# A recurrent scan with a mixture of experts on one core: expert numbers put into PE's registers amid the preceding tile's products, and a new order of the front's steps, of the second scan pass and of the loads

## The chip, the cores and the metric

The kernel runs on one core of one Trainium2 chip. The metric is the device time in microseconds of one execution, as the median over several. The engines are PE (TensorE: matrix products and transposes), DVE (VectorE), ACT (ScalarE), POOL (GpSimd) and SP (which here only issues transfers). Each has its own instruction stream, which it works off in order, and they meet only over semaphores: an instruction waits until a counter has reached a value, and others raise it.

## The reference

The input is x of 2 sequences with 2048 positions of 256 values: 4096 rows, 32 tiles of 128. The first part is a recurrence over time with a layer norm behind it, the second a gated expert layer with a layer norm behind it.

```
# part 1
xB = einsum('bsd,nd->bsn', x, B)
state = tanh(state @ A.T + xb_t)                  # over all positions, states kept
out = einsum('bsn,dn->bsd', states, C) + D * x
attn = layernorm(out + x) * gamma + beta
x = layernorm(x + attn)
# part 2: 8 experts in 2 groups, one group chosen, of it the best 2 experts
scores = sigmoid(x @ router_weight.T);  choice = scores + correction_bias
group = argmax over groups of the sum of the two largest choices
topk = the two best experts of that group;  w = scores[topk] / sum
routed = sum over the two of w * ((silu(x @ w_gate[e]) * (x @ w_up[e])) @ w_down[e])
shared = (silu(x @ sw_gate) * (x @ sw_up)) @ sw_down
x = layernorm(x + routed + shared)
```

## The kernel before, in words

*Scan.* The 4096 positions are cut into 128 chunks of 32 positions that run side by side, so a step of the scan is one matrix product for all chunks (`scan_step`: `drive` puts the B product of the next step into a PSUM bank, the A product is added, ACT takes the tanh). A first pass over 32 steps gives each chunk's starting state, and a second pass of 32 steps, from those, gives the states. During the first pass PE also turns the tiles of x. At step `WMAX_AT` it turns the maxima of the weights that DVE has found, from which come the powers of two by which the weights are scaled before they are split into two f16 parts.

*Front.* The 32 tiles are 8 groups of 4. Every engine walks through one list of tokens, `PLAN`, made by `plan()`, and does those that are its own; so the list sets the order on each engine, and semaphores do the rest. For a group g (with halves n = 2g and 2g+1):

- `A` (PE, `project`): C and D products into PSUM. `M` (DVE, `first`): their statistics. `r` (POOL): root. `S` (DVE, `scaled`), `B` (DVE, `normed`): scale, add the residual, statistics. `R` (POOL): root.
- `X` (ACT, `second`, two halves): second norm and rounding to f16. `Y` (DVE, `low`): the low f16 part. `T` (PE, `turn_x2`): transposes. `K` (ACT, `keep_x2`): copy out of PSUM.
- `L` (PE, `logits`), `Q` (ACT, `squash`), `D` (DVE, `choose`: which two experts), `P` (PE, `ranks`), `E` (DVE, `slots` and `weigh`: the row's place in the sorted list, and its weights), `V` (POOL, four scatters of the rows to DRAM).
- the shared expert, for each half: `U` (PE, `up`), `s` (ACT, `silu`), `H` (DVE, `inner`), `W` (PE, `down`), `Z` (DVE, `add_shared`). All `W` write one bank, so `down(n)` waits for `Z` n-1.

Before, tokens of groups 0 and 1 were put between steps of the second scan pass by a table (`early`), and then period p took `A M r S B R X` of group p, `Y` to `Z` of group p-1, and `P E V` of group p-2.

*Expert tiles.* Rows are sorted by their pair of experts. `N` (DVE, `table`) makes a table that gives for each of up to 43 tiles its first row (`tabR`) and its two experts (`tabE`). SP loads the rows of each tile from DRAM. In iteration i of the list PE does `u` (`up_tile`) of tile i-1, `v` (`turn_h`) of i-2, `t` (`turn_tile`) of i, `d` (`down_tile`) of i-3; ACT does `us` (`silu_tile`) of i-1, `ve` (`keep_h`) of i-2, `te` (`keep_tile`) of i, and then the final scaling `o`. Buffers and banks are double. For a pair of tiles in `ENDS` the last norm is done together: `rr` is POOL's root chain and `os` its scatter of finished rows. The number of an expert is data, so the address of its weights comes from a register of PE that `value_load` fills from SBUF: for both ranks in `up_tile` and again in `down_tile`, each time before the first product:

```
def pair_of(j):
    return [pe.value_load(tabE[0:1, r, j:j + 1], min_val=0, max_val=E - 1) for r in range(2)]
```

Behind the tiles stand slow paths that run only if the chunks' states have not met, and are not run here.

## Time and profile before

| | us |
|---|---|
| median of 3 runs (461.68 to 467.6) | 463.37 |
| profiled execution, its own time | 460.74 |
| its span, first to last instruction | 459.0 |
| PE busy | 299.2 (65%) |
| DVE busy | 236.1 (51%) |
| ACT busy | 155.3 (34%) |
| POOL busy | 139.3 (30%) |
| mean granted TensorE clock | 0.904 of full speed |

The rows further down come from one profiled execution. A row of the timeline or of the chain names a start and a duration in us, the engine, the line of the kernel and what was written from what; in brackets stands the idle time of the engine before it, and what ended it. PEld is PE's loading of weights into the array, PEldq its sequencer's own instructions, which don't count as busy. "issue" is time in which nothing that the profile shows was waited for. The granted clock is 1.00 at 2.4 GHz and 0.50 at 1.2 GHz; a value between is a mean over both.

### The profile page before, as it was taken

To read this page: it belongs to the slowest core of one execution; us is meant where nothing else is said; L and a number is where in the kernel's file an instruction comes from. 1 tells how busy PE (TensorE), PEld (TensorE's weight loads), DVE (VectorE), ACT (ScalarE), POOL (GpSimd) and SP (SyncE) were. 2 spreads that over 40 slices of the span, in tenths; PEclk is the share of its full clock that TensorE was granted. 3 is DMA by queue.
4 is the path that set the end of the run, shared out by engine and by line. 5 is a ranking of instruction groups with operands and counts; after the bars stand their busy time and mean duration, and the time that the engine had idled before them with its cause. 6 is when DMAs were issued, how large, how long until landed. Compare 5 with 4: busy or idle time off the path is not lost.

```text
span 459.0 us, 7930 instructions
## 1 busy us (share of the span) xinstructions
PE 299.2 (65%) x2237; PEld 238.5 (52%) x2237; DVE 236.1 (51%) x928; ACT 155.3 (34%) x354; POOL 139.3 (30%) x241
## 2 busy tenths in 40 slices
PE   6889988737466667665603766667666666766640
PEld 5789977635354546454502645455554545555430
DVE  3259944384948676686491244444344444434440
ACT  2444246123232423324101243443534344353420
POOL 2200111051615152342330024333342333334353
PEclk9999999997887978888755799999999999999995
DMA  6994000010202020211227413223222323300000
GB/s 210 311 361 164 1 0 1 0 66 29 95 0 96 0 95 1 94 43 52 94 94 212 118 33 108 72 81 98 82 76 85 101 71 88 87 22 33 28 5 1
DMA packets 21002, 36.82 MB, mean 80 GB/s; under 512 B 3028, under 2 KB 9693, under 8 KB 20960
## 3 DMA queue, kind: packets, MB, share of 16 engines
q1 hardware_dynamic: 16336, 23.50, 17.6%
q0 software_dynamic: 4624, 12.79, 7.4%
q8 instruction: 23, 0.38, 0.3%
q14 instruction: 19, 0.16, 0.1%
HBM read 20.00 MB, written 17.71 MB: 82 GB/s over the span
## 4 chain that ended last, share of the span: by engine, by line
PE 58%; issue 19%; DVE 7%; ACT 5%; SPq 4%; DMA 3%; POOL 2%; POOLq 0%; DVEq 0%; ACTq 0%
PE bank L657 15%; PE bank L678 10%; PE bank L610 7%; PE bank L622 5%; PE bank L516 4%; PE bank L521 3%; PE bank L557 3%; PE bank L554 3%; PE bank L569 2%; PE bank L633 2%; PE bank L669 2%; ACT xT L797 2%; DMA rows<-in_L_attn_x_dram 2%; SPq L420 1%; DVE rows L1169 1%
## 5 line engine op out<-in xcount | busy, mean ns | idle before, releaser
L657 PE MATMUL bank<-w,xTt 128*128 x516 | 66.8, 281 | 29.3 <-issue 29.3
L657 PEld LDWEIGHTS bank<-w,xTt 128*128 128x128 f16 x516 | 47.2, 100 | 53.2 <-issue 46.5
L678 PE MATMUL bank<-wd,thT 128*128 x172 | 49.3, 410 | 34.6 <-issue 34.6
L1362 POOL TENSOR_TENSOR rstd<-mv,eps 128x2 f32<-128x2 f32 (+2 forms) x39 | 10.0, 258 | 203.3 <-DVE mv L1202 95.4
L821 ACT ACTIVATE tsg<-bank,g_un 128x256 f32<-128x256 f32 x43 | 20.4, 474 | 117.7 <-PE bank L657 117.7
L1395 POOL DMA_INDIRECT out_dram<-xT,where x43 | 44.1, 1025 | 44.4 <-ACT xT L833 36.2
L1188 DVE SCALAR_TENSOR_TENSOR th_<-bank,tw,tsg 128x128 f32<-128x128 f32 x86 | 26.2, 346 | 59.1 <-ACT tsg L821 45.4
L678 PEld LDWEIGHTS bank<-wd,thT 128*128 128x128 f32 x172 | 29.6, 192 | 44.4 <-issue 42.0
L622 PE MATMUL bank<-wd,h 128*128 128x256 f32 x64 | 23.2, 496 | 35.3 <-issue 15.2
L1381 POOL DMA_INDIRECT xs_dram<-rows,slot_i x32 | 33.8, 1056 | 40.8 <-DVE rows L1094 27.9
L1196 DVE TENSOR_TENSOR xT<-bank,xT 128x256 f32<-128x256 f32 x43 | 18.3, 424 | 53.9 <-PE bank L678 53.9
L516 PE MATMUL bank<-xT,BT 128*128 128x128 f32 x256 | 40.3, 281 | 0.0
L610 PE MATMUL bank<-xT,w 128*128 128x256 f16 x192 | 36.3, 364 | 0.0
L1366 POOL TENSOR_TENSOR rstd<-rstd,neghalf 128x2 f32<-128x2 f32 (+2 forms) x39 | 34.9, 894 | 0.6
L516 PEld LDWEIGHTS bank<-xT,BT 128*128 128x128 f32 x256 | 34.5, 196 | 0.1
L622 PEld LDWEIGHTS bank<-wd,h 128*128 128x128 f32 x64 | 13.3, 230 | 40.4 <-DVE h L1163 23.3
L815 ACT ACTIVATE xTt<-bank 128x512 f16<-128x512 f16 x43 | 25.7, 598 | 21.1 <-PE bank L633 20.2
L797 ACT ACTIVATE xT<-bank 128x1024 f16<-128x1024 f16 x16 | 16.4, 1024 | 41.8 <-PE bank L569 41.8
L610 PEld LDWEIGHTS bank<-xT,w 128*128 128x128 f16 x192 | 25.2, 133 | 9.5 <-issue 1.6
L633 PE MATMUL bank<-ident,xT 128*128 128x128 f16 x172 | 17.4, 226 | 14.4 <-DMA xT<-xs_dram 14.4
L833 ACT ACTIVATE xT<-xT,rstd 128x256 f32<-128x256 f32 x43 | 23.7, 604 | 7.9 <-POOL rstd L1372 7.9
L809 ACT ACTIVATE sg<-bank,g_un 128x256 f32<-128x256 f32 x16 | 7.6, 474 | 49.3 <-PE bank L610 49.3
(180 smaller groups left out, 531.5 us busy)
## 6 DMA issues: line engine op xcount, KB each, us to landing
xT<-xs_dram SPq DMA_DIRECT2D x43, 262.0 KB, 3.0
rows<-in_L_attn_x_dram SPq DMA_DIRECT2D x7, 512.0 KB, 7.2
xs_dram<-cmp SPq DMA_DIRECT2D x1, 3144.0 KB, 12.9
...
out_dram<-xT,where POOLq DMA_INDIRECT x43, 2.4
...
xs_dram<-rows,slot_i POOLq DMA_INDIRECT x32, 2.8
...
```

What stands on the lines that cost most here:

```text
L516: pe.matmul(ps_scan[s % 2][:, 0:P], BT[:, k, :], xT[:, k, tile, :], start=(k == 0), stop=False)
L610: last = pe.matmul(ps_gu(n)[:, i * 2 * P:(i + 1) * 2 * P], w16[:, pw, E, k, i, :], cols[:, px, k, :], start=(m == 0), stop=(m == 3 * KT - 1))
L622: last = pe.matmul(ps_y[:, t * DM:(t + 1) * DM], h[:, n % 3, t * P:(t + 1) * P], wd[:, E, :], start=True, stop=True)
L633: last = pe.transpose(ps_tx(j)[:, a, k, :], row[:, a, k * P:(k + 1) * P], ident16[:, :])
L657: last = pe.matmul(ps_tu(j)[:, r, :, :].rearrange("p w i -> p (w i)"), xTt[:, j % 2, 2 * px + k, :], w16[:, pw, bass.ds(e, 1), k, :, :].re ...
L678: last = pe.matmul(ps_ty(j), thT[:, j % 2, r, :], wd[:, bass.ds(e, 1), :].rearrange("p o d -> p (o d)"), start=(r == 0), stop=(r == 1))
L797: nc.scalar.activation(x2cols(g)[:, :, :, half * 2 * P:(half + 1) * 2 * P], x2_turn[:, :, :, :], ACT.Copy).then_inc(x2_kept, 1)
L815: nc.scalar.activation(xTt[:, j % 2, :, :], ps_tx(j).rearrange("p a k t -> p (a k) t"), ACT.Copy).then_inc(tx_kept, 1)
L1188: stt(th_[:, j % 2, r, :], ps_tu(j)[:, r, 1, :], tw[:, j % 4, r:r + 1], tsg[:, j % 2, r, :], ALU.mult, ALU.mult).then_inc(th_ready, 1)
L1366: ins = nc.gpsimd.tensor_tensor(scale[:, 1, :], scale[:, 0, :], neghalf[:, 0:n], ALU.pow)
L1381: nc.gpsimd.indirect_dma_start(out=xs_dram, out_offset=bass.IndirectOffsetOnAxis(ap=slot_i[:, l:l + 1], axis=0), in_=rows[:, l, :], in_off ...
L1395: nc.gpsimd.indirect_dma_start(out=out_rows, out_offset=bass.IndirectOffsetOnAxis(ap=where[:, j:j + 1], axis=0), in_=trow(j)[:, DM:2 * DM] ...
```

## The change

1. *Registers.* `pair_of` is gone. `know(j)` loads one of the two expert numbers of tile j. Only for the first tile both are loaded at the start of `up_tile`; every other tile's numbers are loaded in `up_tile` of the tile before, one ahead of the fourth of six products of either rank. `down_tile` uses the same registers.
2. *Plan.* The second scan pass is interleaved with the steps of groups 0 and 1 and nearly the whole of period 2, one short piece of the list ("atom") after each scan step. The order within a period is new. `weigh` has a token of its own, `w`, directly behind `D`. `A` of the next group stands at the end of a period. The check that the chunks have met is moved out of the scan to the end of period 4.
3. *Banks.* All shared ups use bank 6 and wait for the inner product of the half before; before, they took banks 0 and 1 in turn.
4. *Ends.* Tiles are paired until at most one is left, so the last three tiles end as a pair and one, and not as three.
5. *Loads and preparation.* New order of SP's transfers (vectors, C and router weights before the third group of x; x groups ahead of the weights; D late), of DVE's weight preparation and residual sums, of the D work on POOL, and the two steps at which PE turns the weights' maxima (19 and 21 instead of 15 and 19).

```diff
-        while len(js) > 3:
+        while len(js) > 1:
...
-        early = {4: [("A", 0), ("M", 0), ("r", 0)], 5: [("S", 0), ("B", 0), ("R", 0)], 12: [("A", 1), ("M", 1), ("r", 1)],
-                 15: [("X", 0, 0)], 17: [("X", 0, 1)], 19: [("Y", 0, 0), ("Y", 0, 1), ("S", 1)],
-                 20: [("T", 0, 0), ("K", 0, 0), ("B", 1), ("R", 1)], 22: [("T", 0, 1), ("K", 0, 1)], 24: [("L", 0), ("Q", 0)],
-                 25: [("D", 0)], 27: [("X", 1, 0)], 29: [("X", 1, 1)]}
-        for i in range(L):
-            put(("scan", i), *early.get(i, []))
...
+        steps = [("scan", i) for i in range(L)]
+
+        def scan(n=1):
+            put(*steps[:n])
+            del steps[:n]
+
+
+        scan(4)
+        put(("A", 0), ("M", 0), ("r", 0), ("S", 0), ("B", 0), ("R", 0))
+        scan(4)
+        put(("A", 1), ("M", 1), ("r", 1), ("S", 1))
+        scan(3)
+        put(("X", 0, 0))
+        scan(2)
+        put(("X", 0, 1), ("Y", 0, 0), ("T", 0, 0), ("K", 0, 0), ("Y", 0, 1))
+        scan(1)
+        put(("T", 0, 1), ("K", 0, 1), ("B", 1), ("R", 1))
+        for atom in ([("U", 0), ("s", 0)], [("L", 0), ("Q", 0), ("H", 0)], [("U", 1), ("s", 1), ("D", 0), ("w", 0), ("H", 1)],
+                     [("W", 0), ("Z", 0)], [("X", 1, 0)], [("A", 2)], [("X", 1, 1)], [("W", 1), ("Z", 1)]):
+            scan()
+            put(*atom)
+
+        def period(p):
 
             g, o = p - 1, p - 2
-            tiles = list(tiles)
-
-            def some(k, of):
-                for it in tiles[len(tiles) * k // of:len(tiles) * (k + 1) // of]:
-                    put(*it)
-            if p < G:
-                put(("A", p), ("M", p), ("r", p))
-            if g < G:
-                put(("Y", g, 0), ("T", g, 0), ("K", g, 0), ("Y", g, 1))
-            if 0 <= o < G:
-                put(("P", o), ("E", o))
-                put(*[("V", o, t) for t in range(T4)])
-            some(0, 4)
-            if p < G:
-                put(("S", p))
-            if g < G:
-                put(("T", g, 1), ("K", g, 1))
-                shared(2 * g)
-            if p < G:
-                put(("B", p), ("R", p))
-            some(1, 4)
-            if g < G:
-                put(("H", 2 * g), ("L", g), ("Q", g))
-                put(("W", 2 * g))
-                shared(2 * g + 1)
-                put(("D", g), ("H", 2 * g + 1), ("W", 2 * g + 1), ("Z", 2 * g))
-            some(2, 4)
-            if p < G:
-                put(("X", p, 0), ("X", p, 1))
-            if g < G:
-                put(("Z", 2 * g + 1))
-            some(3, 4)
-
-        queue = []
-        for n in range(2):
-            shared(n)
-            put(("H", n), ("W", n), ("Z", n))
-        for p in range(2, G + 2):
-            take = queue[:len(queue) // (G + 2 - p)] if p < G + 1 else queue
-            queue = queue[len(take):]
-            period(p, take)
-            for c, (g, _) in enumerate(CHECKS):
-                if g == p - 2:
-                    loads(c)
-                    queue += list(iterations(c))
-        for it in queue:
-            put(*it)
+            n = 2 * g
+            on, end = p < G, p >= G
+            atoms = []
+            if on:
+                atoms.append([("M", p), ("r", p)])
+            atoms += [[("P", o)], [("Y", g, 0), ("T", g, 0), ("K", g, 0)], [("Y", g, 1), ("T", g, 1), ("K", g, 1)]]
+            atoms.append([("E", o)] + [("V", o, t) for t in range(T4)])
+            if on:
+                atoms.append([("S", p)])
+            atoms += [[("U", n), ("s", n)], [("L", g), ("H", n), ("Q", g)], [("U", n + 1), ("s", n + 1)]]
+            if on:
+                atoms.append([("B", p), ("R", p)])
+            if end:
+                atoms += [[("W", n), ("D", g)], [("H", n + 1)], [("w", g), ("Z", n)], [("P", g), ("W", n + 1)],
+                          [("E", g), ("Z", n + 1)] + [("V", g, t) for t in range(T4)]]
+            else:
+                atoms += [[("W", n), ("H", n + 1)], [("D", g), ("w", g)], [("W", n + 1)]]
+                if p + 1 < G:
+                    atoms.append([("A", p + 1)])
+                atoms += [[("X", p, 0), ("X", p, 1)], [("Z", n)], [("Z", n + 1)]]
+            return atoms
+
+        for p in range(2, G + 1):
+            for atom in period(p):
+                if steps:
+                    scan()
+                put(*atom)
+            if p == 4:
+                put(("meet", 0))
...
-            return bank[n % 2 if n < two_banks else 0]
+        ps_gu = bank[6]
...
-        TURN_C_AT, WMAX_AT = 5, 15
+        TURN_C_AT, WMAX_AT = 5, 19
...
-            sp.dma_start(D_bc[:, :], D.partition_broadcast(P)).then_inc(D_in, 16)
-            sp.dma_start(D_col[:, :], D.rearrange("(k p) -> p k", p=P), allow_slow_non_contiguous=True).then_inc(D_in, 16)
-            load_x(2)
-            sp.dma_start(C_sb[:, :, :], C.rearrange("(k p) n -> p k n", p=P)).then_inc(Cr_in, 16)
-            sp.dma_start(rw_sb[:, :], router_weight).then_inc(Cr_in, 16)
-            load_weights(0)
-            load_x(3)
-            load_weights(1)
-            load_x(4)
-            load_x(5)
             sp.dma_start(gamma_bc[:, :], gamma.partition_broadcast(P)).then_inc(vecs_in, 16)
             sp.dma_start(beta_bc[:, :], beta.partition_broadcast(P)).then_inc(vecs_in, 16)
             sp.dma_start(cbias_bc[:, :], correction_bias.partition_broadcast(P)).then_inc(vecs_in, 16)
+            sp.dma_start(C_sb[:, :, :], C.rearrange("(k p) n -> p k n", p=P)).then_inc(Cr_in, 16)
+            sp.dma_start(rw_sb[:, :], router_weight).then_inc(Cr_in, 16)
+            load_x(2)
+            load_x(3)
+            load_weights(0)
+            load_x(4)
+            load_weights(1)
+            load_x(5)
+            sp.dma_start(D_bc[:, :], D.partition_broadcast(P)).then_inc(D_in, 16)
+            sp.dma_start(D_col[:, :], D.rearrange("(k p) -> p k", p=P), allow_slow_non_contiguous=True).then_inc(D_in, 16)
...
-                if n >= 1 and (n >= two_banks or n >= 2):
-                    pe.wait_ge(h_done, n if n >= two_banks else n - 1)
+                if n:
+                    pe.wait_ge(h_done, n)
...
-            def pair_of(j):
-                return [pe.value_load(tabE[0:1, r, j:j + 1], min_val=0, max_val=E - 1) for r in range(2)]
+            pair = {j: [] for j in range(NT)}
+
+            def know(j):
+
+                pair[j].append(pe.value_load(tabE[0:1, len(pair[j]), j:j + 1], min_val=0, max_val=E - 1))
 
             def up_tile(j):
 
                 if j == starts[check_of[j]]:
                     pe.wait_ge(table_ready, check_of[j] + 1)
+                    know(j)
+                    know(j)
...
-                for r, e in enumerate(pair_of(j)):
+                for r, e in enumerate(pair[j]):
                     m = 0
                     for k in range(KT):
                         for pw, px in ((0, 0), (0, 1), (1, 0)):
+                            if m == 3 and j + 1 < starts[check_of[j] + 1]:
+                                know(j + 1)
...
+            dve.wait_ge(vecs_in, 16 * NVEC)
+            residual(0)
+            residual(1)
             dve.wait_ge(Cr_turned, 1)
             nc.vector.tensor_copy(rwT[:, :, :].rearrange("p k n -> p (k n)"),
                                   ps_mats[1][:, KT * P:KT * P + KT * E]).then_inc(Cr_done, 1)
             nc.vector.tensor_copy(CT[:, :, :].rearrange("p k n -> p (k n)"),
                                   ps_mats[1][:, 0:KT * P]).then_inc(Cr_done, 1)
-            def residual(n):
-
-                dve.wait_ge(xT_turned, T4 * (n + 1))
-                tt(xres[:, n * T4:(n + 1) * T4, :], xres[:, n * T4:(n + 1) * T4, :],
-                   beta_bc[:, :].unsqueeze(1).to_broadcast([P, T4, DM]), ALU.add).then_inc(res_done, 1)
-
+            residual(2)
             dve.wait_ge(Cr_done, 2)
             greatest(2)
-            for i in (0, 1):
-                dve.wait_ge(w_in[i], 16 * 2)
-                greatest(i)
+            dve.wait_ge(w_in[0], 16 * 2)
+            greatest(0)
+            residual(3)
+            dve.wait_ge(w_in[1], 16 * 2)
+            greatest(1)
+            residual(4)
             scales()
-            dve.wait_ge(vecs_in, 16 * NVEC)
-            for done, i in enumerate((2, 0, 1)):
-                split(i, done + 1)
-                residual(2 * done)
-                residual(2 * done + 1)
+            split(2, 1)
+            split(0, 2)
+            residual(5)
+            split(1, 3)
...
+                elif kind == "w":
+                    weigh(n)
                 elif kind == "E":
                     slots(n)
-                    weigh(n)
```

In PE's instruction stream, at a tile of the middle. L633 (L628 after) are the transposes of `t`, L637 (L635) the register loads, L678 `d`, L657 `u`; ISA rows are register instructions. Before:

```order
L633 MATMUL bank<-ident,xT 128x128 x3
L637 TENSOR_LOAD tabE [waits z2_done,th_kept]
L637 ISA x2
L637 TENSOR_LOAD tabE
L637 ISA x2
L678 ISA
L678 MATMUL bank<-wd,thT 128x256
L678 ISA
L678 MATMUL bank<-wd,thT 128x256
L637 TENSOR_LOAD tabE [waits th_ready,tx_kept]
L637 ISA x2
L637 TENSOR_LOAD tabE
```

The same place in the change:

```order
L628 MATMUL bank<-ident,xT 128x128 x3
L678 ISA [waits z2_done,th_kept]
L678 MATMUL bank<-wd,thT 128x256
L678 ISA
L678 MATMUL bank<-wd,thT 128x256
L657 ISA [waits th_ready,tx_kept]
L657 MATMUL bank<-w,xTt 128x256 x2
L657 ISA
L657 MATMUL bank<-w,xTt 128x256
L635 TENSOR_LOAD tabE
L635 ISA x2
L657 ISA
```

The four loads of a tile that stood before `d` and `u` have become two, each behind three products of `u`; the waits are now on the register instructions of `d` and `u` themselves.

In DVE's stream, in a period of the front: L1060 ends `choose`, L1163 is `inner`, L1169 `add_shared`, L978 the statistics of `first`. Before:

```order
L1059 TENSOR_REDUCE code<-coded 128x4 [waits choice_step]
L1060 TENSOR_TENSOR pick<-code,codes 128x48 [waits choice_step]
L1163 SCALAR_TENSOR_TENSOR h<-bank,u_un,sg 128x256 [waits down_done,silu_done]
L1169 TENSOR_TENSOR rows<-bank,rows 128x2x256 [waits down_done] x2
L978 BN_STATS st<-bank 128x6 [waits c_done]
```

In the change (all lines are 7 further down; L1096 to L1101 are `weigh`; the `inner` of the same half stands 16 rows further up, before `choose`):

```order
L1067 TENSOR_TENSOR pick<-code,codes 128x48 [waits choice_step]
L1096 TENSOR_SCALAR score<-th 128x32
L1097 TENSOR_TENSOR score<-score,kept 128x32 [waits weigh_step]
L1098 TENSOR_REDUCE total<-score 128x4 [waits weigh_step]
L1099 TENSOR_SCALAR total<-total,u_inv 128x4 [waits weigh_step]
L1100 RECIPROCAL total<-total 128x4 [waits weigh_step]
L1101 TENSOR_TENSOR rows<-score,total 128x4x8 [waits weigh_step]
L1176 TENSOR_TENSOR rows<-bank,rows 128x2x256 [waits down_done] x2
L985 BN_STATS st<-bank 128x6 [waits c_done]
```

`choose` and `weigh` have come between the second `inner` and the first `add_shared` of a group.

In PE's stream, at the end of a period: L610 (L605 after) is `up`, L581 `logits`, L622 (L617) `down`, L554 (L549) the start of `project`. Before:

```order
L581 MATMUL bank<-rw,xT 128x8 x23
L622 MATMUL bank<-wd,h 128x256 [waits zbase_done,h_done]
L622 MATMUL bank<-wd,h 128x256
L610 MATMUL bank<-xT,w 128x256 [waits x2_kept,h_done]
L610 MATMUL bank<-xT,w 128x256 x11
L622 MATMUL bank<-wd,h 128x256 [waits zbase_done,h_done]
L622 MATMUL bank<-wd,h 128x256
L554 MATMUL bank<-CT,states 128x256 [waits scan_tanh,scaled1]
```

In the change:

```order
L605 MATMUL bank<-xT,w 128x256 [waits x2_kept,h_done]
L605 MATMUL bank<-xT,w 128x256 x11
L617 MATMUL bank<-wd,h 128x256 [waits zbase_done,h_done]
L617 MATMUL bank<-wd,h 128x256
L617 MATMUL bank<-wd,h 128x256 [waits zbase_done,h_done]
L617 MATMUL bank<-wd,h 128x256
L549 MATMUL bank<-CT,states 128x256 [waits scan_tanh,scaled1]
```

Both downs of a group now stand behind its second up, and `project` directly behind them.

## Rows read from the trace of the kernel before

**Rows 1.** Busy time by stretch: from:to, length, each engine (instructions), clock, DMA share, GB/s

```profile
0.00:42.46 42.46, 35.03 (x274) 32.97 (x275) 20.94 (x80) 18.05 (x62) 5.43 (x26) 1.00 0.90 283
42.46:82.11 39.65, 35.06 (x279) 31.20 (x278) 24.48 (x75) 16.97 (x47) 5.65 (x12) 1.00 0.00 1
82.11:114.90 32.79, 20.62 (x158) 16.73 (x155) 19.02 (x73) 7.45 (x13) 7.97 (x10) 0.90 0.09 33
114.90:198.20 83.30, 53.16 (x416) 42.37 (x416) 57.21 (x233) 26.02 (x44) 31.21 (x40) 0.84 0.14 53
198.20:243.53 45.33, 19.12 (x168) 14.64 (x168) 31.81 (x124) 9.79 (x16) 16.07 (x18) 0.71 0.21 79
243.53:262.25 18.72, 11.71 (x60) 8.29 (x61) 2.98 (x16) 4.33 (x9) 0.00 (x0) 0.60 0.62 185
262.25:436.13 173.88, 119.08 (x859) 88.61 (x859) 74.59 (x314) 68.76 (x155) 63.10 (x114) 1.00 0.25 70
436.13:459.00 22.87, 5.40 (x29) 3.72 (x29) 5.03 (x20) 3.90 (x8) 9.85 (x21) 0.72 0.02 3
```

**Rows 2.** Line 637: durations in ns (least, median, most), first and last start

```profile
L637 PEldq TENSOR_LOAD <-tabE x172: 293/301/491, 245.0 to 441.6; - x172
L637 PEldq FUSED_REGOPS  x172: 151/151/165, 245.6 to 442.0; - x172
```

**Rows 3.** Timeline of two expert tiles, ACT and PE

```profile
312.72 0.47 ACT L821 ACTIVATE tsg<-bank,g_un 128x256 f32<-128x256 f32 x1 [3.03 <-PE bank L657]
...
313.36 0.60 ACT L815 ACTIVATE xTt<-bank 128x512 f16<-128x512 f16 x1
...
315.56 1.48 PE L657 MATMUL bank<-w,xTt 128*128 x12 [0.54 <-issue]
...
318.05 0.60 ACT L815 ACTIVATE xTt<-bank 128x512 f16<-128x512 f16 x1 [0.23 <-PE bank L633]
```

**Rows 4.** Timeline of the second scan pass, ACT

```profile
50.06 0.28 ACT L769 ACTIVATE states<-bank 128x128 f32<-128x128 f32 x1 [3.90 <-PE bank L521]
50.92 0.28 ACT L769 ACTIVATE states<-bank 128x128 f32<-128x128 f32 x1 [0.58 <-PE bank L521]
...
62.12 1.08 ACT L789 ACTIVATE rows<-w,rstd 128x256 f32<-128x256 f32 x2
```

**Rows 5.** Chain that ended last, a stretch of one period

```profile
135.08 0.76 DVE st L978 x2
...
136.12 0.59 DVE rows L1007
...
137.41 1.03 ACT xT L797
...
138.58 0.71 PE bank L569 x8
```

**Rows 6.** The chain in the last tiles, on POOL

```profile
445.43 0.21 POOL rstd L1362
...
447.27 1.08 POOL out_dram L1395
...
448.38 0.20 POOL rstd L1362
```

**Rows 7.** Timeline of the first scan pass, PE

```profile
24.27 0.44 PE L506 MATMUL bank<-ident,rows 128*128 128x128 f32 x2 [3.25 <-DMA rows<-in_L_attn_x_dram]
```

**Rows 8.** The chain in the period before, DVE

```profile
117.39 0.09 DVE score L1089
...
118.63 1.58 DVE w L986 x4
...
120.33 1.67 DVE w L995 x4
...
123.60 0.38 DVE h L1163
```

**Rows 9.** Timeline of a period, DVE's choose and PE's second down

```profile
145.05 0.18 DVE L1013 SCALAR_TENSOR_TENSOR choice<-th,chbias_bc 128x32 f32<-128x32 f32 x1
...
147.62 0.21 DVE L1060 TENSOR_TENSOR pick<-code,codes 128x48 f16<-128x48 f32 x1
...
151.06 1.10 PE L622 MATMUL bank<-wd,h 128*128 128x256 f32 x4 [1.77 <-DVE rows L1169]
```

46 lines of the change are left out of this document (25 added, 21 removed).

## Prediction

> **What bounds the kernel now.** I read the busy time by stage first [rows 1]. There is a front (two passes of a scan, then groups of four tiles, then a table) up to 243.53 us, and then 43 expert tiles. From 262.25 to 436.13 us 39 tiles pass in 173.88 us, 4.46 us each, at the full granted clock (2.4 GHz); PE is busy for 119.1 of it, DVE for 74.6, ACT for 68.8, POOL for 63.1, the DMA engines at 0.25. No engine is full, so I look for a chain. The register loads of `pair_of` are 172 TENSOR_LOADs of 301 ns, each followed by register arithmetic of 151 ns [rows 2]: four a tile, all in PE's sequencer, which works in order. In the timeline [rows 3] ACT ends the copy of the next tile's rows (L815) at 313.96, and the products L657 that read it start at 315.56: 1.60 us, filled by the two loads of `up_tile`. The products take 1.48 (to 317.04), and the next L815 ends at 318.65. So there is a ring: copy ended, two loads, 12 products, three activations on ACT, copy ended. `down_tile` has two more loads, between the transposes and L678.
>
> In the front the clock is 1.00 through the scans, and 0.84 as a mean of 1.2 and 2.4 GHz in the four periods from 114.90 to 198.20 [rows 1]; these take 20.83 us each, with PE busy 13.3 and DVE 14.3. They too are a chain over engines. The second scan pass takes 39.65 us for 32 steps. A step costs 0.86 (ACT's 0.28 and 0.58 idle), and what stands between two steps is added: `project` 3.3 (an idle of 3.90 instead of 0.58), an `X` half about 1.0 (two L789 are 1.08), a T/K half about as much (K is 1.03, mostly ahead of the next step) [rows 4, 5].
>
> **The tile stage.** *Loads.* One load is at least 0.30 + 0.15 = 0.45 us and at most 0.80, half of the 1.60 [rows 2, 3]. I take 0.64, since what is left of the 1.60 must also hold two hand-overs. The change removes two of four loads and puts the other two behind product 3 of each rank. There they are no longer ahead of the products; but PE has only three of them in hand when a load begins (0.33 us, 12 taking 1.3 and a tail), so it runs dry. The hole is at most the whole load, 0.64, and at least 0.64 - 0.33 = 0.31. Handing three over takes nearly as long as working them, so I take 0.48. The 12 products then take 1.48 + 2 x 0.48 = 2.44.
>
> *The ring after.* Copy ended to first product without a load: 0.14, as from L797's end, 138.44, to the transposes at 138.58 [rows 5]. Products 2.44. Then ACT: 1.24 from its first activation in one tile (312.72 to 313.96), 1.61 from the products' end in the next (317.04 to 318.65) [rows 3]; mean 1.42. Sum 4.0. The sequencer alone would need 4.46 - 2 x 0.64 = 3.2, PE's own work 119.1 / 39 = 3.05: the ring still sets the time, through ACT. Saved 0.46 a tile, 39 x 0.46 = 17.9 us. Holes of 0.31 and 0.64 make the ring 3.7 and 4.3, savings of 30 and 6.
>
> *The first tiles*, 243.53 to 262.25, have the clock at 0.60 [rows 1]. At 1.2 GHz three products take 0.65, as long as a load, so the holes nearly close and most of the 1.3 of two loads is saved, two to three times: 2.8, between 1.5 and 4.
>
> *The end.* The last three tiles are single ends; from the root chain of one (445.43) to that of the next (448.38) are 2.95 us, the send's 1.08 among them [rows 6]. With tiles 40 and 41 as a pair one root chain (1.9) goes, and the sends of 38 and 39 no longer stand behind it. PE's last tiles lose three pairs of loads, in part under the same chain. Of 22.9 us I take 4.3; 2 to 5.
>
> **The front.** *Loads.* PE waits 3.25 us for x rows in the first pass [rows 7]: the fifth group, which stood behind both gate and up weights. It now stands ahead of the 1.15 MB of up weights, which at 0.283 MB/us [rows 1] are 4 us: this wait goes. The sixth group stays behind as many bytes as before, and PE comes to it 3.2 sooner, with part of four steps as slack: some 1.5 of wait returns. Net 1.8, between 0 and 3. The scale products move from step 15 to 19, and wait for the up weights' maximum; the sixth group of x, for which step 16 waits, is issued behind those weights, so I count them as there; if not, PE and the scan stop. D lands later, but D_diag is needed only by project 0, in the second pass, and costs nothing. `residual` moves forward into DVE's waits for weights; that is the cover for project 0 a step earlier, and without it Y 0 and with it the scan come late by up to a project, 3.3. On POOL only the D work moves behind the iotas, which nothing waits for here.
>
> *The second pass* now also holds project 2 (3.3), two T/K halves (2.0), four shared-expert ups (12 products each, 1.3 less the step's slack of 0.2: 4.4), two downs (1.8), logits and ranks (0.7): 12.2 more, 51.9 if nothing overlaps. Project 2 on PE lies beside X 1.0 on ACT, and others likewise; I take 50. In exchange the stretch from the pass's end to the end of `first(3)`'s statistics, 82.11 to 114.90, shrinks to the rest of one period: B 3.27, H 0.5, D 2.8, w 1.24, Z 0.6, down 1.1, project 3.3, the last statistics 1.04 [rows 5, 8, 9], together 13.9, of which 2 lie in the pass. So 72.4 us become 62: 10.4 saved, 6 to 14.
>
> *The periods.* In the new order DVE does H 2g+1, D, w and only then Z 2g. `down` 2g+1 waits for that Z; project p+1 is queued behind this down on PE, and `first(p+1)` on DVE waits for project. The chain at full clock: statistics 1.04 (135.08 to 136.12), Y 0.6, T 0.7, K 1.03, T 0.7, up 1.3, silu 0.5, H 0.5, B 3.27, H 0.5, D 2.8 (145.05 to 147.83), w 1.24, Z 0.6, down 0.15 + 1.10, project 3.3. Sum 19.3. Before, D lay under the second up, and w under no wait of PE's. PE idles from the end of down 2g to Z 2g, about 5 us, where the same down now waits 1.77 [rows 9]. What follows at 1.2 GHz is down and part of project: 1.5 to 2.5. So 21.4 against 20.83: four periods cost 2.3 more; 19.5 to 23 gives -5 to +9.
>
> *The last group and the table*, 198.20 to 243.53, 45.3 us: w is done ahead of ranks, and slots ahead of the last Z, so the last scatter need not wait for w and slots (1.24 and about 1.0). I take 1.9 saved; -1 to 5.
>
> Sum: 1.8 + 10.4 - 2.3 + 1.9 + 2.8 + 17.9 + 4.3 = 36.8 us, from the profiled execution's span of 459.0 to 422.2. That execution took 460.74, 1.7 more than its span, and is 2.6 below the median of 463.37, whose three runs spread over 6; with 1.7 and half of 2.6 this gives **425 us**. Of the gain the sequencer and its ring are 21, the front 12, the end 4.
>
> **Rivals.**
> 1. *The front gives back what it gains.* The wait of some 5 us before down 2g+1 is followed by all of down and project at 1.2 GHz, and T and up after the wait for the statistics too: 19.3 + 2.5 + 1.7 = 23.5 a period, and the last group as much later. For it: clock 0.84 in the periods against 1.00 in the scans [rows 1]. Against: PE is dense from down through project. The four periods cost 10.7 instead of 2.3, the last group 3 more: 436. The Trainium skill (TensorE: Matmul & The Clock Gate, Loop structure matters more than you think) says that a long wait inside the loop lets PE go cold, which speaks against this order; by it the time would be this rival's 436.
> 2. *The loads are free amid the products*: PE works on while the sequencer loads. Products 1.48, ring 0.14 + 1.48 + 1.42 = 3.05, so the sequencer's 3.2 sets it: 39 x 1.26 = 49 saved instead of 18, 394. Against: the sequencer stops at `up_tile`'s start until the copy has ended, so nothing is queued ahead, and each product's weights are addressed from registers computed behind the load. The Trainium skill (Advanced Engine Details and Errata, Sequencer Loop) has it that other engine instructions can be read and queued while a control instruction executes; by that it would be 394. No row here has products behind a load that could show it.
> 3. *The loads only change place*: holes of 0.64 and slower handing over, the ring stays near 4.46 and the tile stage gives nothing: 443. For it: ACT's part of the ring is untouched, and both loads are still in it.
> 4. *The other side*: a load amid an accumulation waits until the products under way have drained. Each then costs 0.64, a product's 0.28 and a hand-over of 0.14 with no lead, 1.06: products 3.6, ring 5.2, 0.7 a tile or 28 us lost, against 19 gained elsewhere: 472. It decides against the kernel from a ring of 4.95 on (19 / 39 = 0.49 above 4.46). Against: in [rows 2] the loads' median is 301 and the least 293 ns, and the loads of `up_tile` stand directly behind L678's products; a drain would spread them.
>
> **How the numbers follow.** The forecast 0.62; rival 1 0.18; rival 2 0.05; rival 3 0.08; 1 and 3 together (454) 0.03; rival 4 0.04. Inside the forecast the unknown costs reach from holes of 0.31 (-12) to holes of 0.64 (+12) and periods of 23 (+7), not all at one end. To leave out no more than 2 in 10 I take in rival 1 and stop short of rival 3: 409 to 441. Faster by over 2% (about what a measurement of this kernel can tell from no change) 0.92, within 2% 0.04, slower 0.04.
>
> **What would show it.** 86 TENSOR_LOADs instead of 172; L657's 12 products in 2.2 to 2.8 us instead of 1.48, in three bursts; a tile in 4.0 us; no idle time before L678 that is put down to issue. In the front: no 3 us wait for x; the second pass's end near 91 us; a DVE sequence h, choose, weigh, Z with PE's down waiting 5 us for it in each period of 21.4. The forecast is wrong if the ring is under 3.5 (rival 2) or over 4.3 (rival 3), or if the first expert tile's transposes come after 240 (rival 1) or before 224.

## The result and the profile after

The changed kernel takes 435.54 us (median of 4 runs, 434.05 to 436.16) against 462.52 for the kernel before, run on the same chip: a ratio of 0.943, 95% interval 0.938 to 0.948. The forecast was 425 with a range of 409 to 441. So the sign and the range were right, and the middle was 10.5 us too low. The profiled execution has a span of 434.1 us and a mean granted clock of 0.885 of full speed, against 459.0 and 0.904.

The stages of the changed kernel, busy time by stretch with the columns of [rows 1]:

```profile
0.00:41.69 41.69, 35.39 (x274) 33.55 (x275) 24.95 (x83) 18.05 (x62) 6.84 (x26) 1.00 0.86 275
41.69:91.75 50.06, 46.51 (x405) 42.04 (x405) 32.53 (x111) 20.39 (x54) 11.71 (x18) 1.00 0.09 34
91.75:105.20 13.45, 7.64 (x39) 6.34 (x37) 7.18 (x40) 3.36 (x7) 1.70 (x4) 0.75 0.00 0
105.20:196.80 91.60, 52.29 (x416) 43.99 (x416) 57.09 (x235) 26.12 (x44) 30.72 (x40) 0.80 0.13 48
196.80:242.88 46.08, 19.22 (x160) 14.28 (x161) 30.49 (x116) 9.89 (x16) 15.81 (x18) 0.66 0.22 77
242.88:258.88 16.00, 12.11 (x61) 7.77 (x62) 2.78 (x15) 4.31 (x9) 0.00 (x0) 0.61 0.76 218
258.88:414.40 155.52, 124.39 (x860) 80.36 (x858) 74.38 (x312) 66.58 (x155) 63.09 (x114) 1.00 0.27 78
414.40:434.10 19.70, 5.13 (x29) 3.62 (x29) 5.50 (x21) 3.80 (x8) 8.68 (x17) 0.72 0.04 9
```

They stand against [rows 1] line by line: first pass, second pass, what lies from there to the end of `first(3)`, four periods, last group and table, first tiles, 39 tiles, end. The sum of the forecast, beside the measured stretches (us saved):

| term | forecast | measured |
|---|---|---|
| first scan pass | 1.8 | 0.8 (42.46 to 41.69) |
| second pass and the stretch behind it | 10.4 | 8.9 (72.4 to 63.5) |
| four periods | -2.3 | -8.3 (83.3 to 91.6) |
| last group and table | 1.9 | -0.8 (45.3 to 46.1) |
| first expert tiles | 2.8 | 2.7 (18.7 to 16.0) |
| 39 tiles | 17.9 | 18.4 (173.9 to 155.5) |
| end | 4.3 | 3.2 (22.9 to 19.7) |
| sum | 36.8 | 24.9 |

The ring of the tiles in the timeline of the changed kernel, PE and ACT; this answers to [rows 3]:

```profile
302.24 0.50 PE L657 MATMUL bank<-w,xTt 128*128 x3
...
303.13 0.83 PE L657 MATMUL bank<-w,xTt 128*128 x6 [0.39 <-issue]
...
304.34 0.50 PE L657 MATMUL bank<-w,xTt 128*128 x3 [0.38 <-issue]
...
304.88 0.47 ACT L822 ACTIVATE tsg<-bank,g_un 128x256 f32<-128x256 f32 x1 [2.78 <-PE bank L657]
...
305.51 0.60 ACT L816 ACTIVATE xTt<-bank 128x512 f16<-128x512 f16 x1
...
306.25 0.50 PE L657 MATMUL bank<-w,xTt 128*128 x3
```

The 12 products come in bursts of three, six and three, with a hole in front of the second and the third. They run from 302.24 to 304.84, 2.60 us instead of 1.48. ACT's three activations end at 306.11, and the next products start 0.14 later. A tile takes 4.01 here, 3.99 as a mean. Line 635, which is 637 of [rows 2], has half the loads, at the same duration:

```profile
L635 PEldq TENSOR_LOAD <-tabE x86: 295/302/488, 242.9 to 411.7; - x86
```

What PE and ACT waited for in the changed kernel (us in total, times, longest):

```profile
PE bank L617 <- DVE rows L1176: 39.9, 7, 7.0
PE bank L657 <- issue: 30.2, 78, 0.6
...
ACT th L803 <- remote: 17.6, 6, 3.8
```

L617 is `down`, L1176 is Z. The first line is the wait that the forecast foresaw at 5 us a period, behind choose and weigh. The third is one that it did not have: in six groups ACT stood waiting for the logits although PE's last product of them had ended. This wait for a semaphore that comes late is called the lag below. The kernel before has it too (L802 is the same tanh), 8.1 us in four groups:

```profile
ACT th L802 <- remote: 8.1, 4, 2.4
```

Three of these groups lie in its four periods, and the periods with the lag (20.6 to 20.9 us) are no longer than the one without it (21.2). In the changed kernel both waits are in the chain that ended last, here one period of it (start, us, what):

```profile
109.61 0.47 ACT sg L810
110.08 2.69 another core or an unknown queue
...
112.81 1.52 another core or an unknown queue
...
114.87 0.48 DVE h L1170
115.35 0.11 DVE choice L1020
...
119.29 0.61 DVE rows L1176
...
120.04 2.05 PE bank L617 x4
122.09 0.85 PE bank L549 x2
...
127.56 0.76 DVE st L985 x2
```

From h at 114.87 over choose and weigh (to 119.29), Z, and `down` at 120.04 to `project` from 122.09 to 127.54: that is the sequence of the forecast. `down` takes 2.05 instead of 1.10 [rows 9], `project` 5.45 where the forecast had 3.3 at full clock, and h comes about 1 us late (DVE was free from 113.8), because the logits' semaphore and that of the second up came late. "remote" in the list of waits and "another core or an unknown queue" in the chain name the same thing, a releaser that the profile doesn't find; the kernel has one core.

### The profile page after: what moved, and what is told of

Its sections match the earlier page's. It is cut to its first block, busy times and chain, and to the rows that moved or that the text cites. A ratio compares the mean times of both kernels' runs of the same rounds, so it can differ in the third digit from the quotient of the medians.

```text
span 434.1 us, 7668 instructions
## 1 busy us (share of the span) xinstructions
PE 302.7 (70%) x2237; PEld 231.9 (53%) x2237; DVE 234.9 (54%) x928; ACT 152.5 (35%) x354; POOL 138.6 (32%) x237
## 4 chain that ended last, share of the span: by engine, by line
PE 55%; DVE 14%; issue 12%; SPq 5%; ACT 4%; another core or an unknown queue 4%; DMA 3%; POOL 1%; POOLq 1%; DVEq 0%; ACTq 0%
PE bank L657 19%; PE bank L678 9%; PE bank L549 4%; PE bank L552 4%; PE bank L617 4%; PE bank L511 3%; SPq L415 3%; PE bank L516 3%; PE bank L605 2%; PE bank L628 2%; PE bank L669 2%; PE bank L564 2%; DVE rows L1176 1%; ACT xT L798 1%
## 5 line engine op out<-in xcount | busy, mean ns | idle before, releaser
L657 PE MATMUL bank<-w,xTt 128*128 x516 | 80.5, 282 | 35.0 <-issue 30.2
L657 PEld LDWEIGHTS bank<-w,xTt 128*128 128x128 f16 x516 | 39.7, 99 | 80.1 <-issue 74.5
L617 PE MATMUL bank<-wd,h 128*128 128x256 f32 x64 | 23.9, 510 | 39.9 <-DVE rows L1176 39.9
L678 PE MATMUL bank<-wd,thT 128*128 x172 | 47.7, 401 | 0.2 <-ACT thT L828 0.2
L617 PEld LDWEIGHTS bank<-wd,h 128*128 128x128 f32 x64 | 14.6, 253 | 44.2 <-issue 42.2
L798 ACT ACTIVATE xT<-bank 128x1024 f16<-128x1024 f16 x16 | 16.4, 1022 | 62.0 <-PE bank L564 62.0
L1375 POOL TENSOR_TENSOR rstd<-rstd,neghalf 128x2 f32<-128x2 f32 (+2 forms) x38 | 34.0, 896 | 0.6
L816 ACT ACTIVATE xTt<-bank 128x512 f16<-128x512 f16 x43 | 25.7, 598 | 18.7 <-PE bank L628 18.7
L678 PEld LDWEIGHTS bank<-wd,thT 128*128 128x128 f32 x172 | 29.8, 193 | 2.9 <-issue 0.6
L605 PE MATMUL bank<-xT,w 128*128 128x256 f16 x192 | 27.5, 300 | 2.9 <-DVE h L1170 2.5
L628 PE MATMUL bank<-ident,xT 128*128 128x128 f16 x172 | 17.4, 226 | 12.7 <-DMA xT<-xs_dram 12.7
L552 PEld LDWEIGHTS bank<-D_diag,xT 128*128 128x128 f32 x128 | 23.7, 230 | 3.0
L549 PE MATMUL bank<-CT,states 128*128 128x256 f32 x64 | 24.2, 467 | 0.0
```

The costliest lines, as they stand in the source:

```text
L549: pe.matmul(dst, states[:, g * T4 + t, :], CT[:, :, :].rearrange("p k d -> p (k d)"), start=True, stop=False, skip_group_check=True)
L552: last = pe.matmul(dst[:, k * P:(k + 1) * P], xT[:, k, g * T4 + t, :], D_diag[:, k, :], start=False, stop=(k == KT - 1), skip_group_check= ...
L605: last = pe.matmul(ps_gu[:, i * 2 * P:(i + 1) * 2 * P], w16[:, pw, E, k, i, :], cols[:, px, k, :], start=(m == 0), stop=(m == 3 * KT - 1))
L617: last = pe.matmul(ps_y[:, t * DM:(t + 1) * DM], h[:, n % 3, t * P:(t + 1) * P], wd[:, E, :], start=True, stop=True)
L628: last = pe.transpose(ps_tx(j)[:, a, k, :], row[:, a, k * P:(k + 1) * P], ident16[:, :])
L657: last = pe.matmul(ps_tu(j)[:, r, :, :].rearrange("p w i -> p (w i)"), xTt[:, j % 2, 2 * px + k, :], w16[:, pw, bass.ds(e, 1), k, :, :].re ...
```

## The experiments

Kernels of one call shared a chip and the runs of the kernel before: the first four (before 458.55 us), the next four (462.80), the next three (464.41), the last (460.48). Times are medians of 4 or 5 runs, or single runs where said. The parts of a profile (ring, periods, waits) are those of one execution of each kernel. A ratio to the kernel before carries from one call to another, where a difference of times does not.

**Run 1: the loads back at the heads.** Before each group of products two loads again, and none amid them:

```diff
-                for r, e in enumerate(pair[j]):
+                for r, e in enumerate(pair_of(j)):
...
-                            if m == 3 and j + 1 < starts[check_of[j] + 1]:
-                                know(j + 1)
...
-                for r, e in enumerate(pair[j]):
+                for r, e in enumerate(pair_of(j)):
```

> The changed kernel with one part undone: all four register loads of a tile stand again at the heads of its two groups of products, as in the kernel before; the front's new order, the loads of the inputs and the ends in pairs stay. Ring theory (two of four loads gone, the other two in holes of 0.55 us): the 39 tiles take 4.46 us each again instead of 3.99, so 18 us, the first tiles 2 to 3 more and the end about 1.5 more; the stage before the first expert tile is unchanged (first tile's transposes at 243 +- 1.5). Time 435.5 + 22 = 457, between 454 and 460. Rival (the tile stage got faster through something else of the change, above all the ends in pairs, which halve the root chains on POOL): the ring stays near 4.0 with four loads, the time under 445.

Measured: 451.69 us, ratio 0.986 (0.981 to 0.991), under the 454 to 460 expected. The ring is 4.45, from 253.6 (fourth tile) to 427.0 (last), the products take 1.48 again, and the end takes 20.6 instead of 19.7. PE's waits are back as they were (34.6 and 29.3 us before):

```profile
PE bank L678 <- issue: 34.6, 42, 1.1
PE bank L657 <- issue: 29.1, 43, 2.4
```

So the tile stage's gain is the registers': the ratio goes from 0.938 (the changed kernel in the next call) to 0.986, 22 us of 460. Run 4, in the same call and with the tiles of the changed kernel, is 22.1 under this run. At the end of the kernel the loads are 0.9 of the 3.2 us; the other 2.3 are left for the ends in pairs, which were not undone alone. One thing was not expected, and made the time miss its range: the stage before the first tile, whose code is unaltered, was 7 us shorter than in the changed kernel's own profile (236.0 instead of 242.9), and the lag was not in it.

Without the lag the four periods show what else is in them: they take 23.1, 21.0, 23.1 and 21.2 us. `down` takes 2.05 in each and `project` 4.5 to 5.3. The long ones have besides the first shared up at 1.2 GHz, here the first and the second period's in the chain:

```profile
106.68 2.57 PE bank L605 x12
...
129.47 1.32 PE bank L605 x12
```

**Run 2: the loads behind the down products.**

```diff
-                    know(j)
-                    know(j)
+                    for i in range(j, j + 3):
+                        know(i)
+                        know(i)
...
-                            if m == 3 and j + 1 < starts[check_of[j] + 1]:
-                                know(j + 1)
...
                 last.then_inc(ty_done, 1)
+                if j + 3 < NT:
+                    know(j + 3)
+                    know(j + 3)
```

Since a tile's numbers are now loaded three tiles ahead, those of the first three tiles are loaded together, six loads at the start of the first `up_tile`.

> The changed kernel with the two loads of a tile moved out of the up products to behind L678's products of an earlier tile, the down products, which take about 1.1 us of PE's time and for which nothing waits long. The 12 products L657 then have no load amid them. Theory A (the sequencer loads while PE still works on products it has in hand): products 1.48 us instead of 2.6; the loads begin when the last down product is handed over, about 0.3 to 0.5 us before it ends, and the next products start 0.8 to 1.0 later than the copy would let them; ring 3.5 to 3.85 us instead of 3.99, 6 to 19 us gained over 39 tiles, time 417 to 430. Theory B (a load waits until the products under way have drained): the loads begin when the down products have ended and take 1.3, ring 4.1 to 4.3, time 439 to 447. Theory C (the loads are not what makes the holes in the products, e.g. the change of expert costs it): products stay at 2.6.

Measured: 395.59 us, ratio 0.865 (0.859 to 0.871), some 35 us under the changed kernel (whose ratio is 0.938 to 0.943), better than any theory had it. In its own call it is 34 under run 4. The ring is 3.13 us. The timeline of one tile (lines are shifted: L656 is the up product, L677 the down product, L818 the copy), and under it the line of the loads in the window 303 to 305.4, times in ns, first and last start:

```profile
302.13 1.48 PE L656 MATMUL bank<-w,xTt 128*128 x12 [0.29 <-issue]
303.45 0.38 PE L668 MATMUL bank<-ident,th_ 128*128 128x128 f32 x2
303.67 0.39 PE L628 MATMUL bank<-ident,xT 128*128 128x128 f16 x4
303.89 1.08 PE L677 MATMUL bank<-wd,thT 128*128 x4
...
305.28 1.48 PE L656 MATMUL bank<-w,xTt 128*128 x12 [0.31 <-issue]
```

```profile
L635 PEldq TENSOR_LOAD <-tabE x2: 301/304/308, 303.7 to 304.4; - x2
```

The down products have register addresses as well, two pieces of arithmetic on them, done before the loads start:

```profile
L677 PEldq FUSED_REGOPS  x2: 46/46/46, 303.5 to 303.6; - x2
```

The first load starts at 303.7, when PE has four transposes and all four down products still to work, until 304.97. The second starts 0.65 later. Both are over just behind 305.0, when PE's work in hand ends too, and 0.1 to 0.2 behind the copy that ends at 304.88. So the sequencer was some 1.25 us ahead of PE, not 0.3 to 0.5 as theory A had it, and 1.3 us of loads cost 0.25: the products start 0.38 after the copy on the mean instead of 0.14. Theory B (a load drains the array) and theory C are out. PE's own stream is now the bound: its array is busy for 110.87 of the 122.1 us of the 39 tiles, and the other 11.2 are these holes of 0.29 behind the loads, for which it waits on no other engine.

**Run 3: Z first.** One step of DVE moved, in four periods:

```diff
-                atoms += [[("W", n), ("H", n + 1)], [("D", g), ("w", g)], [("W", n + 1)]]
+                atoms += [[("W", n), ("H", n + 1)], [("Z", n)], [("D", g), ("w", g)], [("W", n + 1)]]
...
-                atoms += [[("X", p, 0), ("X", p, 1)], [("Z", n)], [("Z", n + 1)]]
+                atoms += [[("X", p, 0), ("X", p, 1)], [("Z", n + 1)]]
```

> The changed kernel with one step moved in each of the four periods: on DVE the shared experts' sum Z 2g stands straight behind H 2g+1, ahead of choose and weigh, as it does nowhere in the two kernels. Theory of rival 1 (the loss in the periods comes from PE waiting 5 to 7 us before down 2g+1 for Z 2g behind choose and weigh, and from down, project and what follows at 1.2 GHz): the wait shrinks to under 2 us, down and project 3.3 to 3.6 us instead of 5.5, a period 17.5 to 19 us instead of 22.9, granted clock of the periods from 0.80 to 0.88 or more; time 416 to 420, 15 to 20 us less. Rival (the periods are bound by DVE's own work, or by the late logits and POOL's scatters, and the wait only moves): periods stay over 21.5 us and the time over 430.

Measured: 404.15 us, ratio 0.880 (0.874 to 0.885), 25.5 under run 4 where 15 to 20 were expected. First tile's transposes at 211.8. The four periods of run 1 (which has the changed kernel's front) and of this run, and this run's wait of PE:

```profile
103.30:191.70 88.40, 52.17 (x416) 43.66 (x416) 56.79 (x236) 26.45 (x44) 30.68 (x40) 0.81 0.13 50
```

```profile
98.90:169.40 70.50, 51.37 (x416) 41.52 (x416) 56.23 (x236) 26.47 (x44) 30.15 (x40) 0.81 0.16 62
```

```profile
PE bank L617 <- DVE rows L1176: 8.9, 7, 1.9
```

A period takes 17.6 instead of 22.1 us. The wait went from 34.7 us in seven (run 1) to 8.9. One `down` of a period, in run 1 and in this run:

```profile
118.49 2.04 PE L617 MATMUL bank<-wd,h 128*128 128x256 f32 x4 [5.82 <-DVE rows L1176]
```

```profile
145.97 1.10 PE L617 MATMUL bank<-wd,h 128*128 128x256 f32 x4 [0.87 <-DVE rows L1176]
```

In the four periods the wait is 5.8 each in run 1 and 1.1 on the mean here: 4.7 less, beside the 4.5 by which a period fell. `down` and `project` behind it are at full clock again (1.10 and 3.7). One part of the expectation was wrong: the mean clock did not rise (0.81 in both). Six of the eight shared ups of the periods now run at 1.2 GHz (2.6 to 2.8 us instead of 1.47), where in run 1 it was two of eight. So it is the wait that costs, and the slow clock has moved to other products.

**Run 4: the scatters behind the roots.**

```diff
-            atoms.append([("E", o)] + [("V", o, t) for t in range(T4)])
+            atoms.append([("E", o)] + ([] if on else [("V", o, t) for t in range(T4)]))
...
-                atoms.append([("B", p), ("R", p)])
+                atoms.append([("B", p), ("R", p)] + [("V", o, t) for t in range(T4)])
```

> The changed kernel with POOL's four scatters of a period moved behind its reciprocal roots R p, so that they no longer run while PE makes the logits and the second shared up. In the changed kernel the logits' semaphore comes 2.3 to 3.8 us later than the last recorded product of L in six groups, and ACT waits for it. Theory D (products of so few columns, or their hand-over, are slow while POOL's indirect DMAs run): the lag falls to about 0.3 us in the groups of the periods, silu 2g+1 and h 2g+1 come 0.9 to 1 earlier, the X halves that wait for R p up to 1 earlier; a period 21.5 to 22.3 instead of 22.9, time 431 to 434. Rival (the lag has another cause, and the scatters have none in it): lag stays over 2 us, time 435 +- 1.5.

Measured: 429.64 us, ratio 0.938 (0.933 to 0.943). Nothing can be read from it. None of the four kernels of this call has the lag, whether its scatters are moved or not, and the period of 22.1 is that of run 1 (22.25 in run 2).

**Run 5: the changed kernel again.**

> The changed kernel itself, beside the others of this call on the same chip, to be the base for them. In the four kernels run so far beyond it the logits' semaphore never came late, though two of them (loads at heads, loads behind down) have its front unaltered; in the changed kernel's own profile it came 2.3 to 3.8 us late in six groups, and so it did in the kernel before. If the lag belongs to the chip or the execution, this run has none, its four periods take 22.0 to 22.3 us instead of 22.9 and the first tile's transposes come at 236 to 238 instead of 242.9; time 428 to 432. If it belongs to the program, the lag and 22.9 are back, time 435 +- 1.5.

Measured: 433.78 us, ratio 0.938 (0.931 to 0.944), within 1% of the first call's 0.943. The lag is there (14.6 us in six groups), and the periods take 22.8. So it is no accident of one execution, and yet the same front ran without it in runs 1 and 2.

**Run 6: both edits.** Runs 2 and 3 together.

> The changed kernel with both edits that gained alone: the two register loads behind the down products (ring 3.13 instead of 3.99) and Z 2g ahead of choose and weigh (period 17.6 instead of 22.2). The two lie in different stages, one before 243 us and one behind. If they add: against the changed kernel on the same chip 34 us from the ring and the tail and 25 from the front, time 366 to 373. If the clock couples them (a denser front leaves a lower or higher clock to the tiles) they do not add, and the time is over 378.

Measured: 372.18 us, ratio 0.805 (0.800 to 0.810), 61.6 under run 5. They add: ring 3.13, period 17.7. The lag is there in five groups (11.3 us).

**Run 7: the loads behind the fifth product.** `m == 3` becomes `m == 5`.

> The changed kernel with its two loads amid the up products one place size further: behind the fifth of six products of each rank instead of the third. Theory H (handing a product to PE takes nearly as long as PE takes to work it, so the lead does not grow): the idle of PE behind the load stays at 0.5 to 0.6 us, the 12 products take 2.5 to 2.7 us, ring 3.9 to 4.05, time within 3 us of the changed kernel. Theory G (PE's sequencer gets ahead with each product, so five in hand cover more of the load than three): holes 0.1 to 0.4, products 1.7 to 2.3, ring 3.1 to 3.7, time 12 to 35 us less.

Measured, one run: 431.43 us, ring 3.96. The products in the timeline:

```profile
302.82 0.73 PE L657 MATMUL bank<-w,xTt 128*128 x5
303.94 0.84 PE L657 MATMUL bank<-w,xTt 128*128 x6 [0.39 <-issue]
305.12 0.28 PE L657 MATMUL bank<-w,xTt 128*128 x1 [0.34 <-issue]
```

Five, six and one, with holes of about the same size: the sixth product comes some 0.57 us later than it would without the load. So theory H holds: more products of this kind give almost no lead. The load starts at 303.2, when PE begins the fifth of the five products; in the changed kernel it starts as late, at 302.4, when PE begins the third of three. The line of the up products of the changed kernel has the sequencer's address arithmetic beside them:

```profile
L657 PE MATMUL bank<-w,xTt x516: 272/273/421, 244.7 to 415.6; 128*128 x172
L657 PEldq FUSED_REGOPS  x344: 46/46/51, 244.6 to 415.2; - x172
```

Each tile's 12 products carry 8 pieces of it. Run 2, where no load stands amid them, shows how fast the sequencer gets through them (one tile; first and last start):

```profile
L656 PE MATMUL bank<-w,xTt x12: 272/273/280, 305.3 to 306.5; 128*128 x12
L656 PEldq FUSED_REGOPS  x8: 46/46/51, 305.2 to 306.1; - x8
```

It gains about 0.3 us on PE over all twelve, so some 0.1 over three or five (an estimate from these two lines). Together with run 2 this settles what a load costs. Of its 0.65 to 0.77 us (0.65 from load to load in run 2; 1.55 for two at the heads of run 1, from 1.69 less 0.14), a hole of 0.56 is left amid the up products. Behind the down products two loads leave 0.24. The addresses of these come from registers as well, but they are done by 303.6 (run 2), and give PE 1.08 us of work.

**Run 8: both edits and Y first.** The steps Y g stand ahead of `first(p)` in each period.

> As the kernel with both edits, with one more step moved in the periods: Y g (both halves, the low parts of the second input) ahead of first p on DVE. In the kernel with Z first, PE stood from the end of project (97.6) to the transposes of g (99.6) and its first shared up came at 102.2 and at 1.2 GHz, since Y stood behind first's statistics, though the X that it reads had ended at 97.0. If that idle is what bounds the period now: transposes and up 1.5 to 3 us earlier and at full clock, a period 15.5 to 16.8 us instead of 17.6, time 4 to 9 us under the kernel with both edits. If first p with the root, the scaling and the normalisation behind it bound the period (they start 1.3 later here): no gain, or up to 1.3 us a period, 5 in all, lost.

Measured: 364.09 us, ratio 0.788 (0.782 to 0.794), 8.1 under run 6. The period is 15.4, though the lag is there in four groups (8.7 us).

**Run 9: with the scatters moved as well.** And the first tiles' loads are spread:

```diff
             def turn_tile(j):
+                if j == 0:
+                    pe.wait_ge(table_ready, 1)
+                if j < 2:
+                    know(j)
+                    know(j)
...
                 last.then_inc(tx_turned, 1)
+                if j == 1:
+                    know(2)
+                    know(2)
```

> The last kernel (loads behind the down products, Z first, Y first) with two more steps: POOL's scatters of a period behind its roots R p, and the register loads of the first three tiles spread (tile 0's ahead of its transposes, while its rows are still under way; tile 1's and 2's beside ACT's copies) instead of six in a row ahead of the first products. In the last kernel the first products started at 208.24, 3.2 us behind the end of the copy at 205.06: this goes, 3 us gained. The scatters: if they are what delays the logits' semaphore (1.0 to 2.7 us in five of its groups), a period is up to 1 us shorter, 4 to 5 us in all, time 357 +- 3. If not, only the 3 us of the loads, 361 +- 2.

Measured: 364.28 us, ratio 0.783 (0.775 to 0.792), no better than run 8 and above both expectations. The start of the tiles, from the first transposes to the fourth tile's products, fell from 17.4 to 12.8, but the period rose from 15.4 to 16.4. In the timeline a copy of `keep_x2` waits while PE's transposes, which it reads, have ended at 145.84:

```profile
145.22 0.62 PE L564 MATMUL bank<-ident,rows 128*128 128x128 f16 x8 [0.25 <-DVE rows L1019]
145.46 1.15 POOL L1395 DMA_INDIRECT xs_dram<-rows,slot_i  x1 [0.30 <-issue]
147.41 1.02 ACT L803 ACTIVATE xT<-bank 128x1024 f16<-128x1024 f16 x1 [3.16 <-remote]
```

The lag has left the logits of the periods and stands at the products that now end while the last scatter runs.

**Runs 10 and 11: the scatters moved in the changed kernel, and beside it the changed kernel.** One run each.

> The changed kernel with the scatters behind R p once more, since on the chip of its first run no kernel had the lag at the logits' semaphore. It tells something only where the changed kernel, run beside it, has the lag. Theory D (the scatters cause it): the lag over 2 us in six groups there, and 0.3 us or none here from the first period to the last, four periods 0.5 to 0.9 us shorter each. Rival (the execution causes it): the lag is here too, in the same groups.

> The changed kernel itself again, as the base for the scatters' run beside it. Either theory: the lag of the logits' semaphore over 2 us in six groups and periods of 22.8, if this chip or execution has it, else none and 22.1; time 428 to 436.

Measured: 435.65 and 433.65 us. Here the changed kernel has the lag, and the pair can be read. The logits of the same group, first without the edit, then with it (PE's products, POOL's last scatter, ACT's tanh):

```profile
130.63 0.75 PE L576 MATMUL bank<-rw,xT 128*128 128x8 f16 x24
...
133.36 0.98 POOL L1390 DMA_INDIRECT xs_dram<-rows,slot_i  x1 [0.30 <-issue]
...
135.14 0.29 ACT L803 ACTIVATE th<-bank,l_un 128x32 f32<-128x32 f32 x1 [3.84 <-remote]
```

```profile
132.24 0.75 PE L576 MATMUL bank<-rw,xT 128*128 128x8 f16 x24
...
133.02 0.29 ACT L803 ACTIVATE th<-bank,l_un 128x32 f32<-128x32 f32 x1
```

In all, the tanh waits 17.4 us in six groups without the edit, and 2.1 in one with it: in the last group, whose scatters the edit leaves beside the logits. A period takes 22.25 instead of 22.8. The whole time did not fall (the single runs differ by 2 us the other way): the first pass ended 1.5 later in this run, and its ring was 4.06 instead of 3.99. So theory D holds in this pair of single executions: the lag goes with the scatters, and the edit is worth nothing that could be measured.

**Run 12: the scatters back.** Run 9 without its scatter edit.

> The kernel with loads behind the down products, Z first and Y first, with the loads of the first three tiles spread as in the last kernel, but with the scatters where the changed kernel has them. In the last kernel the start of the tiles (first transposes to the fourth tile's first product) fell from 17.4 to 12.8 us, and the periods rose from 15.4 to 16.4. Theory: the period rose because the scatters behind R p now keep POOL from the next period's root r until they end (it waits for them, and S and all behind it with it); with the scatters back the period is 15.2 to 15.7 again and the start stays at 13, time 358 to 361. If the period's rise belongs to the chip of that run, it can be 16.4 here too, time 362 to 366.

Measured: 352.00 us, ratio 0.765 (0.762 to 0.769), the fastest kernel of the study and under the 358 to 361 expected. The period is 14.5 and the start of the tiles 11.3. The four periods:

```profile
99.70:157.80 58.10, 42.29 (x414) 36.39 (x411) 55.42 (x236) 25.86 (x44) 27.79 (x40) 0.97 0.20 75
```

DVE is busy for 55.4 of 58.1 us: it is the bound now, and the clock is 0.97. Between run 9 and this one the ratio fell by 0.018, some 8 us. How much of that the place of the scatters costs is not shown, since this run also lacks the lag: run 8, with the scatters where they are here and with the lag, has a period of 15.4, run 9 16.4. My reason for the cost was wrong: in run 9 POOL's root r of `first(p)` ran at 115.69, straight behind the statistics that ended at 115.6, while the last scatter had ended at 113.5. What stands in run 9 is the late copies. And this run has its scatters beside the logits and no lag at all.

## Why the prediction was right or wrong, point by point

**The 39 tiles: right in mechanism and size.** Holes 0.56 for a forecast 0.48, products 2.60 for 2.44, hand-over 0.14 as read from [rows 5]. ACT's part came out at 1.27 where I took the mean 1.42 of two alternating values [rows 3]; the two errors cancel, ring 3.99 for 4.0. Run 1 shows that the gain is the registers'. The estimate of a load at 0.64 was close to the 0.65 from load to load in run 2. Rival 3 (ring near 4.46) fell with it.

**Rival 2 was put too low, in a form that the kernel did not test.** It did not happen amid the up products: the ring is 4.0, not 3.2. But its mechanism is real: in run 2 the sequencer loads while PE works for 1.25 us on what it was handed, and the ring is 3.13, under the 3.2 that I took for the sequencer's floor. The rule of the Trainium skill (Advanced Engine Details and Errata, Sequencer Loop) lets the sequencer queue other engine instructions while a control instruction executes; what run 2 shows is the other order, instructions queued ahead of the load being worked during it, and that agrees with the page's steps of reading and queueing. The lead must first be gained: run 7 shows that five up products gain hardly more than three. My argument against rival 2 (nothing queued ahead, weights addressed from registers) held for the place that the change chose. Its second half is not the reason: the down products have register addresses too, and behind them the loads are nearly free.

**Rival 4 fell.** No load waits for a drain: run 2's first load starts with some eight products unfinished on PE, and in the changed kernel the holes are shorter than a load.

**The front, to the end of first(3): right.** 50.06 us for the second pass (50 forecast). The loads gave 0.8 instead of 1.8: the 3.25 us wait [rows 7] is gone, but 2.8 us are still waited for x in three places, the longest 1.6, where it was 3.8 in two. None of the edits of this stage was undone alone.

**The periods: right in mechanism, under-priced.** 91.6 us, where the forecast had 85.6. The wait before down 2g+1 is there, 5.8 us in each of the four periods of run 1. The price of the slow work behind it, "down and part of project: 1.5 to 2.5", came out: in run 1 `down` costs 0.95 more than at full clock and `project` 0.8 to 1.6 more, 2.1 together on the mean. What failed are two other terms of the sum. It has "project 3.3" where run 3 shows 3.7 at full clock, and it has the first shared up of a period at full clock, "up 1.3", while that up took 2.6 to 2.8 in two of the four periods of run 1. The two periods without a slow up take 21.0 and 21.2, which is under the 21.4 of the forecast; the two with one take 23.1, and the mean is 22.1. In the changed kernel's own profile a period is 22.9: `down` and `project` take some 0.4 more there, behind waits of 5.8 to 7.0, and h comes late by the lag. Against the forecast that is 3 us in four periods without the lag, and 3 more in the profile that has it.

Run 3 shows that the order of Z caused the loss: moved, it gives 4.5 us a period. Of the Trainium skill (TensorE: Matmul & The Clock Gate, Loop structure matters more than you think) the trace agrees that a long wait inside the loop is followed by slow products; run 3 adds that the wait itself was the larger part of the loss (4.7 less waiting beside 4.5 us of period).

**Rival 1 came nearer than the forecast.** It had 23.5 a period, with `up` slow behind the wait for the statistics, and 436 in all, against 22.9 and 435.5. By the prediction's own sign ("or if the first expert tile's transposes come after 240 (rival 1)") the forecast was wrong in the front: they came at 242.9. That the whole time still lies in the range is owed to the rival having been taken into it. And the rival's number is met partly by luck, since its sum has no lag in it: without the lag the transposes came at 236.0 and 237.9 (runs 1 and 2), and run 4, whose tiles are those of the changed kernel, took 429.64, between 425 and 436.

**The last group and the table: wrong in sign.** 46.1 us instead of 43.4. In runs 1 and 2, without the lag, the same code takes 44.3 and 43.3. So the forecast was near for an execution without the lag; what the clock of 0.66 (0.71 before) took of the rest was not tested. The 45.3 of before have the lag in them too, in one group.

**The end: 3.2 of 4.3.** Two parts, 0.9 from the loads (run 1) and 2.3 left for the pair of ends. I had let the pairing count a root chain of 1.9 and the sends; the loads gave less, probably since there they lie under that chain.

**The sum.** 36.8 forecast, 24.9 measured: 6.0 of the difference lie in the periods, 2.7 in the last group, 1.5 in the pass and behind it, 1.1 at the end, 1.0 in the first pass, against 0.4 gained.
